# Linear attention with bias products on 96 rows and its residual on VectorE, and both halves of the products with values in one block

## What is computed

```python
q = heads(x @ Wq.T + bq); k = heads(x @ Wk.T + bk); v = heads(x @ Wv.T + bv)
g = jax.nn.sigmoid(heads(x @ Wg.T + bg))
q = jax.nn.elu(apply_rope(q)) + 1.0
k = jax.nn.elu(apply_rope(k)) + 1.0
# per chunk of 64 tokens
S = S + einsum('bhtd,bhte->bhde', ki, vi); Z = Z + ki.sum(axis=2)
num = einsum('bhtd,bhde->bhte', qi, S)
den = einsum('bhtd,bhd->bht', qi, Z)[..., None] + 1e-06
out = gi * num / den
x = layernorm(x + out @ Wo.T + bo)
```

## Time and profile before

| | us |
|---|---|
| median of 3 runs | 1009.85 |
| lowest, highest | 1009.58, 1013.3 |
| the profiled execution | 1009.48 |
| its span, first to last instruction | 1007.7 |
| TensorE busy | 963.4 |
| VectorE busy | 642.2 |
| ScalarE busy | 444.5 |
| GpSimd busy | 312.0 |

### The profile page before, as it was taken

One profiled execution on the slowest core, in us unless ns is written; L12 is line 12 of the kernel. 1 busy time (PEld: TensorE's weight loads), 2 busy tenths in 40 slices (PEclk: granted clock), 3 DMA queues, 4 the chain that ended last, 5 costly groups with the idle time before them and its releaser, 6 DMA issues.

```text
span 1007.7 us, 18735 instructions
## 1 busy us (share of the span) xinstructions
PE 963.4 (96%) x6131; PEld 757.6 (75%) x6131; DVE 642.2 (64%) x1466; ACT 444.5 (44%) x870; POOL 312.0 (31%) x514
## 2 busy tenths in 40 slices
PE   7999999999999999999999989998999998999994
PEld 5788886688888888888887745567787775888883
DVE  3776777656555555555557567768777865555555
ACT  4777786422233222323222333325777784333331
POOL 1133123344444444444445130110000106344430
PEclk9999999999999999999999999999999999999998
DMA  8000000255433333333332000011111120554401
GB/s 282 19 17 18 2 2 1 65 169 179 144 127 115 110 112 110 116 110 110 110 113 88 0 10 1 1 34 38 30 33 36 34 67 21 126 154 109 111 20 42
DMA packets 37356, 75.20 MB, mean 75 GB/s; under 512 B 7116, under 2 KB 18360, under 8 KB 37154
## 3 DMA queue, kind: packets, MB, share of 16 engines
q1 hardware_dynamic: 37006, 74.18, 25.5%
q0 software_dynamic: 288, 0.23, 0.2%
HBM read 67.21 MB, written 2.40 MB: 69 GB/s over the span
## 4 chain that ended last, share of the span: by engine, by line
PE 87%; DVE 7%; issue 2%; ACT 1%; POOL 1%; DMA 0%; SPq 0%; POOLq 0%; DVEq 0%; ACTq 0%
PE ps L1053 34%; PE ps L1079 17%; PE ps L424 5%; PE ps L674 3%; PE ps L519 3%; PE ps L431 3%; PE ps L913 2%; PE ps L511 2%; PE ps L550 2%; PE ps L791 1%; PE ps L846 1%; PE ps L841 1%; DVE ps L1748 1%; PE ps L810 1%; PE ps L888 1%
## 5 line engine op out<-in xcount | busy, mean ns | idle before, releaser
L1053 PE MATMUL ps<-shared 128*128 128x512 f32 x1560 | 377.8, 391 | 1.2 <-POOL shared L2096 0.7
L1053 PEld LDWEIGHTS ps<-shared 128*128 128x128 f32 x1560 | 292.9, 188 | 65.4 <-issue 4.9
L1489 ACT ACTIVATE shared<-pT 128x512 fp32r<-128x512 f32 x130 | 82.2, 632 | 286.5 <-DVE pT L1909 286.5
L2109 POOL CAST shared<-wraw 128x512 fp32r<-128x512 f32 (+1 forms) x130 | 92.2, 709 | 293.1 <-PE ps L1079 279.5
L1912 DVE TENSOR_TENSOR al<-pT,shared 128x512 fp32r<-128x512 f32 x130 | 118.8, 914 | 90.8 <-ACT shared L1489 90.8
L1901 DVE TENSOR_TENSOR e<-e,ps 128x512 f32<-128x512 f32 x130 | 89.3, 687 | 122.1 <-PE ps L1053 117.8
L1079 PE MATMUL ps<-shared 128*128 128x512 f32 x520 | 160.3, 389 | 0.4 <-DVE al L1912 0.4
L2111 POOL TENSOR_TENSOR shared<-wraw,shared 128x512 fp32r<-128x512 f32 (+1 forms) x130 | 132.1, 1017 | 10.4
L1079 PEld LDWEIGHTS ps<-shared 128*128 128x128 f32 x520 | 97.5, 188 | 21.4 <-DVE al L1912 1.3
L1483 ACT ACTIVATE e<-ps 128x512 f32<-128x512 f32 x130 | 77.7, 597 | 73.4 <-PE ps L1053 73.4
L1909 DVE TENSOR_TENSOR pT<-e,kbd 128x512 f32<-128x512 f32 x130 | 99.9, 769 | 7.1
(11 more groups left out here) (230 smaller groups left out, 1397.8 us busy)
## 6 DMA issues: line engine op xcount, KB each, us to landing
kbd<-combine_C SPq DMA_DIRECT2D x46, 512.0 KB
wraw<-in_C_w SPq DMA_DIRECT2D x48, 384.0 KB, 8.6
kbd<-combine_F SPq DMA_DIRECT2D x15, 512.0 KB
wraw<-in_F_w SPq DMA_DIRECT2D x17, 384.0 KB, 6.9
kbd<-kbd SPq DMA_DIRECT2D x96, 32.0 KB, 1.9
kT<-kbd SPq DMA_DIRECT2D x48, 32.0 KB, 1.8
c_ctx_t<-in_ctx_t SPq DMA_DIRECT2D x1, 1024.0 KB, 9.1
out<-c_x_rows SPq DMA_DIRECT2D x2, 512.0 KB, 3.0
```

The lines of the kernel that those rows point to most:

```text
L1053: mm = pe.matmul(GU[t][s], w[u][:, (c * 2 + s) * P:(c * 2 + s + 1) * P], xx[:, c, t * HALF:(t + 1) * HALF], start=(i == 0), stop=(i == 5))
L1489: act.activation(ah[t][:, :], a2[t], ACT.Copy).then_inc(S("ah"), 1)
L2109: pool.tensor_copy(wh[u][:, lo:hi], wraw[k][:, lo:hi]).then_inc(S("m_wh"), 1)
```

## The change

It makes these edits:

- `values(t - 2, 0)` leaves the end of iteration t of the first pipeline; `values(t - 3, 0)` stands directly ahead of `values(t - 3, 1)` in the next one.
- The bias rows and the row of ones are 96 rows high, rows 1 to 31 and 33 to 95 of the biases being zero.
- `linear_project` has no product of X with the identity. DVE's new `linear_residual` adds X to y while it reads it from its bank; ACT's `linear_z` is gone.
- The gate is Tanh of half the argument, and the division is num * (1 + tanh) * 1 / (2 * den), with the reciprocal taken of 16 columns per batch.
- `numerators` waits for S("D_an") first, and for b < 2 it issues three keep-pace products ahead of its other waits.

```diff
@@ -98,7 +98,7 @@
-        braw = arena[0:33, filled["DE"]:filled["DE"] + 5 * D + P]
+        braw = arena[0:96, filled["DE"]:filled["DE"] + 5 * D + P]
@@ -160,11 +160,11 @@
-        rows33 = shared[2][0:33, 0:5 * D + P]
-        brow = shared[2][0:33, 0:5 * D]
-        ones33 = shared[2][0:33, 5 * D:5 * D + P]
+        rows96 = shared[2][0:96, 0:5 * D + P]
+        brow = shared[2][0:96, 0:5 * D]
+        ones96 = shared[2][0:96, 5 * D:5 * D + P]
         den = sb("den", [P, 16])
-        d2 = sb("d2", [P, D])
+        dinv = sb("dinv", [P, 16])
@@ -606,6 +606,7 @@
                     pe.wait_ge(S("pc"), 8 * B)
                     pe_gate_up(pe, "C", 0, 0, 0, (0,))
                 if lo:
+                    values(t - 3, 0)
                     values(t - 3, 1)
                 if lp:
                     project_values(t - 1)
@@ -640,7 +641,6 @@
                     out_T(t - 3)
                 if lv:
                     second_transposes(t - 2, 1)
-                    values(t - 2, 0)
                 if t == 2 * B + 1:
                     pe.wait_ge(S("sub"), 4 * B - 1)
                     pe_logits(pe, "B", range(4))
@@ -669,7 +669,7 @@
                     pe.wait_ge(S("D_ra"), b)
                     pe.wait_ge(S("D_v"), b)
                 for n, w in enumerate(("wqk", "wgv")):
-                    pe.matmul(ps[:, n, :], ones33[:, :], brow[:, n * HALF:(n + 1) * HALF], start=True, stop=False)
+                    pe.matmul(ps[:, n, :], ones96[:, :], brow[:, n * HALF:(n + 1) * HALF], start=True, stop=False)
                     for k in range(C):
                         mm = pe.matmul(ps[:, n, :], XT[:, k, tok(b)], W["D", w][:, k, :], start=False, stop=(k == C - 1))
                     mm.then_inc(S("D_qkps" if n == 0 else "D_gvps"), 1)
@@ -697,10 +697,12 @@
 
             def numerators(b):
 
+                if b > 0:
+                    pe.wait_ge(S("D_an"), b)
+                if b < 2:
+                    pe_keep_pace(pe, 5, 3)
                 pe.wait_ge(S("D_qf"), b + 1)
                 pe.wait_ge(S("D_gm"), b + 1)
-                if b > 0:
-                    pe.wait_ge(S("D_an"), b)
                 for c in range(C):
                     for n in range(2):
                         for r in range(2):
@@ -722,8 +724,7 @@
                 pe.wait_ge(S("D_at"), b + 1)
                 pe.wait_ge(S("z"), nb("D", b + 1))
                 y_ = ps[:, 6, 0:D]
-                pe.matmul(y_, ones33[:, :], brow[:, 2 * HALF:], start=True, stop=False)
-                pe.matmul(y_, ident[:, :], X[:, b, :], start=False, stop=False)
+                pe.matmul(y_, ones96[:, :], brow[:, 2 * HALF:], start=True, stop=False)
                 for k in range(C):
                     mm = pe.matmul(y_, aT[:, k, :], W["D", "wo"][:, k, :], start=False, stop=(k == C - 1))
                 mm.then_inc(S("y"), 1)
@@ -1257,9 +1258,9 @@
 
                 act.wait_ge(S("D_gvps"), b + 1)
                 if b >= 2:
-                    act.wait_ge(S("D_div"), 3 * (b - 2) + 2)
+                    act.wait_ge(S("D_div"), 3 * (b - 2) + 3)
                     act.wait_ge(S("D_gmps"), b - 1)
-                act.activation(eg[b % 2][:, :], ps[:, 1, 0:D], ACT.Exp, scale=-1.0).then_inc(S("D_eg"), 1)
+                act.activation(eg[b % 2][:, :], ps[:, 1, 0:D], ACT.Tanh, scale=0.5).then_inc(S("D_eg"), 1)
                 act.activation(v3[b % 2], ps[:, 1, D:2 * D].rearrange("p (h w) -> p h w", w=DH0), ACT.Copy)\
                    .then_inc(S("D_v"), 1)
 
@@ -1286,13 +1287,6 @@
                 act.activation(aT[:, :, :].rearrange("p c q -> p (c q)"), MB[:, 0:D], ACT.Copy)\
                    .then_inc(S("D_at"), 1)
 
-            def linear_z(b):
-
-                act.wait_ge(S("y"), nb("D", b + 1))
-                if b >= 2:
-                    act.wait_ge(S("xn"), nb("D", b - 1))
-                act.activation(z[b % 2][:, :], ps[:, 6, 0:D], ACT.Copy).then_inc(S("z"), 1)
-
             def linear_x(b):
 
                 act.wait_ge(S("xtr"), nb("D", b + 1))
...
@@ -1376,8 +1370,6 @@
-                if at(t - 4) is not None:
-                    linear_z(t - 4)
...
@@ -1419,8 +1409,6 @@
-                    if k == 3 and do is not None:
-                        linear_z(do)
...
@@ -1675,20 +1663,26 @@
 
                 dve.wait_ge(S("D_num"), b + 1)
                 num = ps[:, 4:6, 0:D].rearrange("p r (m w) -> p r m w", w=VW)
-                two = [x[:, :].rearrange("p (r m w) -> p r m w", r=2, w=DH0) for x in (eg[b % 2], d2, r2, an)]
+                two = [x[:, :].rearrange("p (r m w) -> p r m w", r=2, w=DH0) for x in (r2, an)]
                 den2 = den[:, :].rearrange("p (r m) -> p r m", r=2)
-                dve.tensor_scalar(den2, num[:, :, :, DH0], 1e-6, None, ALU.add).then_inc(S("D_div"), 1)
+                dve.tensor_scalar(den2, num[:, :, :, DH0], 1e-6, 2.0, ALU.add, ALU.mult).then_inc(S("D_div"), 1)
                 dve.wait_ge(S("D_div"), 3 * b + 1)
+                dve.reciprocal(dinv[:, :], den[:, :]).then_inc(S("D_div"), 1)
+                dve.wait_ge(S("D_div"), 3 * b + 2)
                 dve.wait_ge(S("D_eg"), b + 1)
-                dve.scalar_tensor_tensor(d2[:, :].rearrange("p (h w) -> p h w", w=DH0),
+                dve.scalar_tensor_tensor(r2[:, :].rearrange("p (h w) -> p h w", w=DH0),
                                          eg[b % 2][:, :].rearrange("p (h w) -> p h w", w=DH0), 1.0,
-                                         bc(den[:, :], 2, DH0), ALU.add, ALU.mult).then_inc(S("D_div"), 1)
-                dve.wait_ge(S("D_div"), 3 * b + 2)
-                dve.reciprocal(r2[:, :], d2[:, :]).then_inc(S("D_div"), 1)
+                                         bc(dinv[:, :], 2, DH0), ALU.add, ALU.mult).then_inc(S("D_div"), 1)
                 dve.wait_ge(S("D_div"), 3 * b + 3)
                 if b > 0:
                     dve.wait_ge(S("D_atr"), b)
-                dve.tensor_tensor(two[3], num[:, :, :, 0:DH0], two[2], ALU.mult).then_inc(S("D_an"), 1)
+                dve.tensor_tensor(two[1], num[:, :, :, 0:DH0], two[0], ALU.mult).then_inc(S("D_an"), 1)
+
+            def linear_residual(b):
+
+                dve.wait_ge(S("y"), nb("D", b + 1))
+                dve.tensor_tensor(z[b % 2][:, :], ps[:, 6, 0:D], X[:, b, :], ALU.add).then_inc(S("z"), 1)
+                dve_stats(dve, "D", b, b % 2)
 
             def residual(b):
                 dve.wait_ge(S("y"), nb("E", b + 1))
@@ -1774,7 +1768,7 @@
                 if at(t - 4) is not None:
-                    dve_stats(dve, "D", t - 4, t % 2)
+                    linear_residual(t - 4)
                 if at(t - 2) is not None:
                     linear_out(t - 2)
...
@@ -1811,7 +1805,7 @@
                     if k == 4 and do is not None:
-                        dve_stats(dve, "D", do, do % 2)
+                        linear_residual(do)
...
@@ -2084,7 +2078,7 @@
-            pool.tensor_copy(rows33, braw[:, :]).then_inc(S("brow"), 1)
+            pool.tensor_copy(rows96, braw[:, :]).then_inc(S("brow"), 1)
@@ -2260,7 +2254,7 @@
-    d["D_brow"] = np.zeros((33, 5 * D + P), np.float32)
+    d["D_brow"] = np.zeros((96, 5 * D + P), np.float32)
```

More of the change, by code:

```diff
@@ L1400, in act_linear_cross @@
                 ep, es, ev, ef, el = (at(t - B - n) for n in range(5))
-                if t == B + 1:
-                    linear_z(t - 4)
                 for k in range(STEPS):
```

## The result

The kernel after takes 1001.67 us in the median of five runs (999.82 to 1003.22). Two more runs of the kernel before put its median at 1012.53, and the ratio is 0.990, with a 95% interval of 0.988 to 0.992. That is 10.9 us less where I had forecast 14.1, and 1001.67 lies outside my range of 991.5 to 1000.5. The two profiled executions differ by less: 1001.67 (span 999.9) against 1009.48 (span 1007.7), 7.8 us.

The account below looks back on a forecast made before the run. TensorE was taken to bound the kernel, at full clock nearly throughout. Savings of 12.5 us (D and start of E) and 1.6 (attentions), total 14.1, gave 995.4, forecast as 995.5 with 0.4 for the median; range 991.5 to 1000.5.

Parts of the forecast that it names:

- Steps 1 and 2: Layer D: bias products on 96 rows save 0.8 us per batch, linear_project without the X product 0.62 per batch.
- The first rival: Layer D: 96 rows are no full array, 8.0 us less saved, 1003.5 us; chance 0.10.
- Step 3: Layer D's division: DVE loses about 1.1 us per batch; no steady gain itself, but keeps DVE under the shorter period.
- The fourth rival: Layer D: the edit does nothing, another queue takes over (DVE still 9 us per batch), 1007 us; chance 0.02.
- Step 4: Start of layer D: second numerators 2.6 us earlier, bounds 2.1 and 2.6; keep-pace products cost 0, at worst 0.1 each.
- alternation: Layer D, rival: Tanh and Exp don't share tables, two loads per batch, wholly exposed 1014.7 us; chance slower 0.03.
- Step 5: Layer D: 10.4 us earlier at the last numerators, 1.5 behind them; D and the start of E 12.5.
- Step 6: Attentions: moving the values products together saves 5.7 us less 4.1 of waits, 1.6; bounds 0 and 5.7.
- The second rival: Attentions give nothing or lose, 0 to +1 instead of -1.6 us, 997 to 998; chance 0.14.
- Step 7: POOL's copy of 96 bias rows costs 0, as bound up to 1.2 us more; the longer load is hidden.

Follow-up runs that it names:

- experiment 6: Kernel after with the old exponential gate, 256-column reciprocal and old addresses: 1002.49 us, 5.7 above the kernel after with 960 bytes of padding restoring old addresses.
- experiment 7: Kernel after, padded to old addresses, with only 33 bias rows loaded and copied, the other 63 zeroed by POOL: 997.84 us against 996.82 for the padded kernel.
- experiment 4: Kernel after with every tile of 256 bytes or more placed at a multiple of 256 bytes: 995.42 us, ratio 0.982.

## Why the prediction failed, by its own steps

**The step that failed is an unwritten one**: that a stage without an edit keeps its time. My sum had no term for C and F. It put them at nothing without a reason. The shorter scratch tile moved `al` off its address, and 118 groups lost 0.033 each: 3.9 us. With `al` back the kernel takes 996.7 to 996.8, where I had forecast 995.5, and its distance to the kernel before, 14.8 and 15.8 us by the medians taken beside them, is about the 14.1 of my sum. Why such an address costs time stays open.

**Steps 1 and 2 (rows, linear_project)** hold. The bias product joins its neighbours but for 0.1 ahead of the first of each projection's (0.32 to its successor, where I had 0.22), a projection takes 3.98 (forecast 3.9), linear_project starts its products 0.62 earlier. The first rival, that 96 rows are no full array, is out.

**Step 3 (DVE)** holds: 12.09 busy of 16 us is 5.8 per batch of 7.66 (forecast 5.9). What I called no gain by itself in the steady part costs 5.7 us by the medians if it is left out, the gate with it (experiment 6): it is the condition of the other steps, more than I had thought. The fourth rival, that DVE keeps D at its old period, is out with the period of 7.66.

**Step 4 (start of D)** holds within its bounds. The table load went from the gate to the first exponential, one in all, as ACT's timeline after shows, so no alternation:

```profile
597.32 0.38 ACT L1263 ACTIVATE supT<-ps 128x256 f32<-128x256 f32 x1 [4.34 <-PE ps L674]
...
599.82 1.28 ACT L1273 ACT_TABLE_LOAD   x1
```

Counted from D's first product the first numerators come 1.72 earlier (forecast 1.9) and the second 2.24 (forecast 2.6, bounds 2.1 to 2.6).

**Step 5 (sum of D)**: 10.18 for 10.4. At the start of E one term was mis-sized: 0.57 instead of 1.5 at the second scores. TensorE's and SyncE's rows after, and then SyncE's before, show who is late next:

```profile
651.25 0.61 PE L792 MATMUL ps<-c_ctx_t,arena 128*128 128x128 f32 x4
...
662.48 0.64 PE L842 MATMUL ps<-kT,shared 100*128 100x128 f32 x4 [0.77 <-issue]
...
667.76 0.66 PE L842 MATMUL ps<-kT,shared 100*128 100x128 f32 x4 [0.92 <-DVE shared L1722]
```

```profile
653.77 5.42 SPq L372 DMA_DIRECT2D kbd<-kbd  x8
659.31 1.84 SPq L383 DMA_DIRECT2D kT<-kbd  x3
```

```profile
658.77 5.42 SPq L372 DMA_DIRECT2D kbd<-kbd  x8
664.31 1.84 SPq L383 DMA_DIRECT2D kT<-kbd  x3
```

From E's first key projection to its first scores are 11.23 in both traces (651.25 to 662.48 here; before 656.25 to 667.48, the latter in the earlier trace rows): projection, copy, eleven DMA issues of SyncE and their landing. Before, TensorE arrived just as that chain ended; the last numerators now come 0.9 earlier in relation to it, and wait. From the first scores to the second the forecast held: 5.28 for 6.77, the 1.5 of the division.

**Step 6 (attentions)** holds with its waits: 1.36 for 1.6. This is the second attention after:

```profile
121.83 0.60 PE L519 MATMUL ps<-c_ident,e 128*128 128x128 f32 x4
122.54 1.16 PE L424 MATMUL ps<-supT,arena 128*128 128x128 f32 x8
123.54 0.38 PE L582 MATMUL ps<-c_ident,refT 128*128 128x128 f32 x2
123.85 1.08 PE L550 MATMUL ps<-pT,v 128*32 128x128 f32 x32
124.86 1.14 PE L431 MATMUL ps<-arena,supT 128*128 128x256 f32 x4
```

There are 32 records in one block, 1.01 from its start to the next, where two blocks of 16 were 0.57 each; and project_keys starts 0.71 behind the transposes in place of 0.43, since it waits for ACT's copy, which ends at 122.49: 0.28 lost, where I had 0.40 in this attention. From scores to scores, six periods fell by 0.17 to 0.20 (9.53 to 9.33 in the late part of the first attention, 10.74 to 10.56 around its end). The two before them, 9.31, grew by 0.02 or 0.03, and the four behind them, 9.87 or 9.88, by 0.03 to 0.05, about as I had it for the iterations with fewer transposes and for those where the relus stand ahead of the copy. The second rival, nothing or a loss, is out.

**Step 7 (POOL's copy, longer load)**: the copy holds, 1.82 us with 33 and with 96 rows, and the wait behind it is 0.5 us in both traces. The load is doubtful. I called it hidden because it is issued 300 us ahead of its use. The question was whom it may delay: the weights of the dense products came late beside it, for 0.7 us of TensorE in the profiled execution and 3.9 in the next, which experiment 7 leaves as likely and not shown.

**The rest is spread between executions.** The median before was 1009.85 from three runs and 1011.6 to 1013.0 from 11 to 23 later ones, so 2 to 3 us of my distance to 1001.67 were in the starting point. The start of the program took 19.3 to 21.6 us up to the second scores, in either kernel.

## What to carry to other kernels

A change's diff is not the whole of what it changes: removing or shrinking one tile moves all that are allocated behind it, and an operand that TensorE streams through in a hundred groups can lose 4 us by 64 bytes. After such an edit compare the pace of an untouched steady stage in both traces before looking for causes elsewhere, and allocate the large operands at multiples of 256 bytes, ahead of the scratch tiles; the kernel with all of them there lost nothing by it. And ask of a load that is needed late not when it lands but what it overtakes or delays.

## What the runs showed of the hardware that I had not expected

The start address of an SBUF operand can cost time although it is a multiple of its element. For `al`, at 64 bytes beyond a multiple of 256, it did: TensorE took 4.113 for 4.08 per group with two 512-column fp32r reads of it, 0.033 for both, and VectorE's 512-column fp32r write of it 943 ns for 920. It isn't a rule for every operand: f32 writes of 512 columns by VectorE at such an address, f32 reads of 128 columns by TensorE, transposes at 32 bytes beyond a multiple of 64, and 512-column f32 reads at a multiple of 128 showed nothing (experiment 4). What tells `al` from these, its type, its length or that both engines stream at the same time, and whether the read or the write is what costs TensorE its time, was not tried.

One wait of TensorE can cost more than itself. Behind the 2.07 us wait in the second trace of the kernel after, the granted clock was 0.83 over 10 us, and that group and its neighbour took 12.12 for 8.23, which is 3.9 us for a wait of 2.1:

```profile
235.00:245.00 10.00, 10.00 (x46) 8.21 (x45) 5.38 (x8) 3.63 (x6) 1.15 (x2) 1.00 0.59 179
245.00:255.00 10.00, 7.93 (x28) 6.09 (x27) 4.15 (x5) 1.28 (x3) 4.48 (x6) 0.83 0.53 159
```

Some of the spread between executions is of this kind. In the second trace of the kernel before, the start of E took 1.5 us longer than in the first, at a granted clock of 0.75 from 678 to 684 us, behind the same wait of 1.60 for DVE that cost only itself in the first.
